# One order for each engine, key columns twice in the weights, fp32 keys transposed and then split, in a fused four-block kernel

## The reference, cut to what matters

```python
def _L0(x, attn_bias, mask, g_in, null_attn_bias, null_kv, Wq, Wkv, Wo, g_out):
    xn = layernorm(x, g_in)
    q = (xn @ Wq).reshape(b, n, H, DH).transpose(0, 2, 1, 3) * scale
    k, v = split(xn @ Wkv)                      # one head of 64 each
    k, v = concat([null_kv[0], k]), concat([null_kv[1], v])
    sim = einsum('bhid,bjd->bhij', q, k) + concat([null_attn_bias, attn_bias])
    sim = where(causal or masked, -max, sim)
    out = einsum('bhij,bjd->bhid', softmax(sim), v)
    return layernorm(out.reshape(b, n, H * DH) @ Wo, g_out)

def _L1(...):   # the same, but q and k are l2-normed and scaled, and the bias is
    h = silu(ln(silu(ln(pos @ w0 + b0, g0)) @ w1 + b1, g1)) @ w2 + b2
    bias = h[i - j + n - 1]

def _L2(hidden, g, wt, wg, w_gate, w_up, w_down, sw_gate, sw_up, sw_down):
    scores = softmax((hidden @ wt.T + repeat(g @ wg.T)) / 2);  top 2 of 8, renormed
    y_all = einsum('etm,emh->eth', leaky(x @ w_gate) * (x @ w_up), w_down)
    return sum of the chosen y_all * weight + leaky(x @ sw_gate) * (x @ sw_up) @ sw_down

x = x + _L0(x, ...); x = x + _L1(x, ...); x = x + _L2(x, ...); x = x + _L3(x, ...)
```

## Time and profile before

| | |
|---|---|
| Runs, us | 355.8, 356.56, 358.19 (median 356.56) |
| Profiled execution, span from first to last instruction, us | 354.29 |
| Median of the runs less that span, us | 2.27 |
| PE busy, us (share) | 326.7 (92%) |
| DVE, ACT, POOL busy, us | 252.7, 245.7, 197.6 |
| PE without work, whole span, us | 27.6 |
| of that in the first 25 us | 5.7 |
| Mean granted TensorE clock | 0.990 |

### The profile page before, as it was taken

One profiled execution on the slowest core, in us unless ns is written; L12 is line 12 of the kernel. 1 busy time (PEld: TensorE's weight loads), 2 busy tenths in 40 slices (PEclk: granted clock), 3 DMA queues, 4 the chain that ended last, 5 costly groups with the idle time before them and its releaser, 6 DMA issues.

```text
span 354.3 us, 7091 instructions
## 1 busy us (share of the span) xinstructions
PE 326.7 (92%) x2276; PEld 247.4 (70%) x2276; DVE 252.7 (71%) x917; ACT 245.7 (69%) x822; POOL 197.6 (56%) x297
## 2 busy tenths in 40 slices
PE   7789999997999999989996899889999899999996
PEld 5676875777686677756685577667767578676885
DVE  4768998795575777858884889578769536477672
ACT  3579886995698688969894889697986922232330
POOL 4591196379527956977596779877953502200000
PEclk9999999998999999999998999999999999999999
DMA  5961202320939401128200202021120200000001
GB/s 178 382 171 42 62 0 64 48 59 1 142 39 150 91 2 37 26 64 345 58 5 2 62 1 61 5 58 31 33 61 2 61 2 0 0 3 0 0 2 59
DMA packets 26653, 21.33 MB, mean 60 GB/s; under 512 B 2436, under 2 KB 25976, under 8 KB 26232
## 3 DMA queue, kind: packets, MB, share of 16 engines
q1 hardware_dynamic: 25624, 20.37, 23.2%
q10 hardware_dynamic: 992, 0.51, 1.1%
HBM read 19.84 MB, written 1.04 MB: 59 GB/s over the span
## 4 chain that ended last, share of the span: by engine, by line
PE 45%; POOL 16%; ACT 13%; DVE 12%; DMA 6%; issue 6%; ACTq 0%; SPq 0%; DVEq 0%; POOLq 0%
PE bank L1422 7%; ACT sb_prob L785 5%; POOL sb_nb L927 5%; POOL sb_oT L933 4%; PE bank L1389 3%; DMA sb_r_rows<-recip_rows 3%; DVE sb_prob L1164 3%; PE bank L1361 3%; PE bank L1414 3%; PE bank L1446 3%; PE bank L1540 3%; PE bank L1536 2%; ACT sb_pT L793 2%; POOL sb_rq L908 2%; PE bank L1502 2%
## 5 line engine op out<-in xcount | busy, mean ns | idle before, releaser
L785 ACT ACTIVATE sb_prob<-sb_prob,sb_low 128x128 f32<-128x128 f32 (+1 forms) x256 | 113.4, 449 | 5.0 <-DVE sb_low L1164 3.9
L793 ACT ACTIVATE sb_pT<-bank 128x512 f32<-128x512 f32 x96 | 54.0, 590 | 10.2 <-PE bank L1414 9.4
L1414 PE MATMUL bank<-sb_ident,sb_prob 128*128 128x128 f32 x384 | 56.4, 281 | 3.4 <-ACT sb_pT L793 1.4
L1414 PEld LDWEIGHTS bank<-sb_ident,sb_prob 128*128 128x128 f32 x384 | 42.2, 141 | 21.2 <-issue 8.3
L1422 PE MATMUL bank<-sb_pT,sb_v_a 128*64 128x512 f32 x192 | 48.3, 609 | 1.9 <-ACT sb_ln L806 1.9
L785 ACT ACTIVATION_READ_ACCUMULATOR sb_prob<-sb_prob,sb_low 128x1 f32 x256 | 49.8, 195 | 0.0
L933 POOL TENSOR_TENSOR sb_oT<-sb_oT,sb_r_rows 128x512 f32<-128x512 f32 x30 | 38.1, 1292 | 13.5 <-DMA sb_r_rows<-recip_rows 12.2
L1164 DVE CUSTOM_DVE_ANT_0 sb_prob<-bank,sb_nb,sb_t 128x128 f32<-128x128 f32 x128 | 38.6, 342 | 9.7 <-PE bank L1389 8.8
L908 POOL TENSOR_TENSOR sb_rq<-sb_ss,sb_minus_half 128x8 f32<-128x8 f32 x16 | 26.4, 1651 | 15.6 <-DVE sb_ss L1131 15.5
L846 ACT ACTIVATE sb_leak<-bank 128x512 f32<-128x512 f32 x20 | 12.0, 598 | 30.2 <-PE bank L1504 30.0
L1446 PE MATMUL bank<-sb_wo,sb_oT 128*128 128x128 f32 x256 | 31.6, 276 | 0.5 <-POOL sb_oT L933 0.4
(11 more groups left out here) (205 smaller groups left out, 772.6 us busy)
## 6 DMA issues: line engine op xcount, KB each, us to landing
sb_r_rows<-recip_rows SPq DMA_DIRECT2D x30, 256.0 KB, 4.1
sb_packed<-in_packed SPq DMA_DIRECT2D x1, 2992.0 KB, 11.9
sb_bias<-in_bias SPq DMA_DIRECT2D x1, 2048.0 KB, 13.3
sb_toep<-bias_table SPq DMA_DIRECT2D x8, 256.0 KB, 9.4
sb_stage<-in_L_cond_Wq SPq DMA_DIRECT2D x2, 512.0 KB, 5.4
sb_bias<-in_bias SPq DMA_DIRECT2D x1, 1024.0 KB, 8.5
sb_wo<-in_L_cond_Wo SPq DMA_DIRECT2D x1, 512.0 KB, 12.4
sb_wo<-in_L_cond_Wout SPq DMA_DIRECT2D x1, 512.0 KB, 7.0
```

The lines of the kernel that those rows point to most:

```text
L785: act.activation(p[:, j], p[:, j], ACT.Exp, scale=-1.0, bias=low[:, buf, half, h:h + 1], accum_out=total[:, buf, half, h:h + 1]).then_inc( ...
L793: act.activation(pT[:, c % PT_SLOTS].rearrange("p j q -> p (j q)"), t_ring.bank("T", s, n)[:], ACT.Copy).then_inc(t_ring.frees("T", s, n), 1)
L1414: ins = pe.transpose(dst[:, j * P:j * P + P], p[:, j % 2, kb * P:kb * P + P], ident[:])
```

## The change

The change has five parts.

1. `AT`, `attention_order` and `ORDER` go. Each engine gets a string of letters, one letter for a kind of step, which gives that engine's own order; the numbers within a kind run up. All engines but SyncE get another order than before. SyncE's loads ahead of the list stay as they are.
2. The weights hold the key columns twice, so `kv` is 208 columns wide in place of 144 (192 in place of 128 for answer 0), and a key arrives twice side by side without a copy. The split of the key-value weights is done in pieces.
3. `kt` transposes the keys in fp32 straight from `sb_kv`, in one step of two transposes in place of two steps of two, and the split into high and low comes behind it: in `ke`, ACT writes the high parts of `sb_k_bd` and `sb_kT` from the bank, DVE the low parts. `sb_k_src`, `sb_kn`, `sb_v_a` and the steps `k_hi` and `k_lo` go. In block 1 a DVE step `k_gain` scales the keys in `sb_kv` in place.
4. `sb_kv` has two buffers, by the answer's parity. `V` reads the values from it. The eviction of `kv` waits for the last `V` of the answer two before.
5. `m_first`, the first step of the experts' down product, becomes part of `m_down`.

```diff
-ORDER = attention_order()
+KV = 3 * DH + H
+QKV = INNER + KV
...
+def in_order(kinds, letters):
+
+    kinds = kinds.split()
+    left = {kind: iter(pieces(kind)) for kind in kinds}
+    named = [kinds[LETTERS.index(letter)] for letter in letters]
+    return [(kind, *next(left[kind])) for kind in named]
...
+ORDERS = {
...
+    "PE": in_order(
+        "xt kv kt q h kvn S T V Z NW ht W table qt m_g m_x m_logits m_weights m_gate m_spread m_down spread",
+        "abcdeddfdgabgdhhgcidghhdighgjhghhkldheiahmhhgjbilhdchggihhggnmhjdihhdhghihdmhhgaijbhhdggichdmhhgghijdhhgai"
...
-    kv = sb("kv", [P, 2, KV])
+    kv = sb("kv", [P, 2, 2, KV])
-    kn = sb("kn", [P, 2, DH])
-    k_src = sb("k_src", [P, 2, 2, 2, DH], F32R)
-    v_a = sb("v_a", [P, 2, 2, DH])
...
-        for kind, s, n in ORDER:
+        for kind, s, n in ORDERS["ACT"]:
...
             if kind == "kv":
                 w.wait_ge(*p_ring.filled("kv", s, 0))
-                if s > 0:
-                    w.wait_ge(t0_made, 2 * s)
-                cols = 2 * DH if s == 0 else KV
-                act.activation(kv[:, :, 0:cols],
+                if s >= 2:
+                    w.wait_ge(t0_made, 2 * (s - 1))
+                    w.wait_ge(*o_ring.filled("V", s - 2, FOURS - 1))
+                cols = 3 * DH if s == 0 else KV
+                act.activation(kv[:, buf, :, 0:cols],
...
-            if kind == "k_hi":
-                w.wait_ge(*p_ring.emptied("kv", s, 0))
-                if lay == 0:
-                    act.activation(k_src[:, :, 0], kv[:, :, 0:DH].unsqueeze(2).to_broadcast([P, 2, 2, DH]), ACT.Copy,
-                                   scale=K_SCALE).then_inc(kv_high, 1)
-                if s >= 2:
-                    w.wait_ge(*o_ring.filled("V", s - 2, FOURS - 1))
-                act.activation(v_a[:, buf], kv[:, :, DH:2 * DH], ACT.Copy)\
-                    .then_inc(kv_high, 1)
...
+                src = t_ring.bank("kt", s, 0)
+                for j in range(2):
+                    rows = slice(j * DH, j * DH + DH)
+                    act.activation(k_bd[rows, 0, j], src[rows, 0:P], ACT.Copy, scale=scale).then_inc(k_high, 1)
+                act.activation(kT[:, buf, 0], src[:, 0:N], ACT.Copy, scale=scale).then_inc(k_high, 1)
...
+            if kind == "ke":
+                scale = K_SCALE if lay == 0 else 1.0
+                src = t_ring.bank("kt", s, 0)
+                w.wait_ge(k_high, 3 * s + 3)
+                for j in range(2):
+                    rows = slice(j * DH, j * DH + DH)
+                    ins = dve.scalar_tensor_tensor(k_bd[rows, 1, j], src[rows, 0:P], scale, k_bd[rows, 0, j].bitcast(F32),
+                                                   ALU.mult, ALU.subtract)
+                ins.then_inc(k_diagonal, 1)
+                dve.scalar_tensor_tensor(kT[:, buf, 1], src[:, 0:N], scale, kT[:, buf, 0].bitcast(F32),
+                                         ALU.mult, ALU.subtract).then_inc(t_ring.frees("kt", s, 0), 1)
...
             if kind == "kt":
-                w.wait_ge(kv_low, s + 1)
-                for part in range(2):
-                    ins = pe.transpose(dst[:, part * P:part * P + P],
-                                       k_src[:, n, part].rearrange("p c d -> p (c d)").bitcast(F32), ident[:])
+                if lay == 0:
+                    w.wait_ge(*p_ring.emptied("kv", s, 0))
+                else:
+                    w.wait_ge(kn_made, s - B + 1)
+                for t in range(2):
+                    ins = pe.transpose(dst[:, t * P:t * P + P], kv[:, buf, t, 0:P], ident[:])
                 ins.then_inc(full, 1)
```

441 lines of the change are left out of this document (123 added, 318 removed).

## The result

In the comparison that goes with the changed kernel it takes 369.65 us (median of four runs, 367.69 to 371.68) and the kernel before 357.38 (355.8 to 358.29): a ratio of 1.036, interval 1.031 to 1.041. It is slower, as forecast, and inside the stated range, but the forecast said +1.5% and it is +3.6%: 369.65 us lies where rival C was put (365 to 372) and not where the forecast's own story was (358 to 366).

The account below looks back on a forecast made before the run. PE was taken to bound the kernel, busy 326.7 of 354.3 us. 354.3 + 9.0 + 0.9 − 1.6 − 7.9 + 5.0 = 359.7 us of span, 2.3 more for the runs: 362.0 us (+1.5%), range 351.5 to 370.

Parts of the forecast that it names:

- rival C: Slower still: all five `W` waits in full and DVE bounding block 0; 367.5 us for the runs, chance 0.24.
- the forecast's own story: Whole kernel: a start that costs ten and is given back in part; 362.0 us, chance 0.49 for 358 to 366.
- The start: First `h` on PE waits for nine small loads until 21.2 us, delaying S.0.2 from 26.90 to 36.1: +9.0 us.
- The clock: PE's idle at the start lowers its granted clock; half of one drop like that at 83 us: +0.9 us.
- PE's own work: On PE, sixteen transposes go (−2.2 us) and 48 `kv` matmuls get 64 columns more (+0.6): −1.6 us.
- Waits that go: PE's waits of `xt` on `norm` (4.6), `kt` on ACT's eviction (2.1) and `kv` on the split (1.2) vanish: −7.9 us.
- Waits that come: PE at `W` waits for the reciprocals' way from `Z` through `scale`, 8.7 us each, at five places: +5.0, between 0 and 8.5.
- ACT and DVE at nothing: Copies leave ACT (about −1.2 us per answer), half the split goes to DVE (+0.5); both costed at nothing.
- Rivals A and B: A: touched waits and both clock drops go, no `W` waits, 353.6 us, 0.19; B: `h` does not wait, 353.1 us, 0.08.

Follow-up runs that it names:

- start2: Changed kernel with the first steps of PE, DVE, ACT and POOL, first `h` among them, in about the sequence of the kernel before: 360.9 us, ratio 1.008.
- best2: start2 with six `scale` steps on POOL and four `W` on PE (with their evictions) moved later: 356.5 us, ratio 0.992 to the kernel before.
- no_rows: Changed kernel, but `scale` multiplies `sb_oT` by itself without waiting for the reciprocals' rows, so the softmax is not normalised: 346.52 us, ratio 0.970.
- w_late: Changed kernel with only four `W` on PE moved later, with their evictions on ACT and DVE: 377.86 us, ratio 1.056 to the kernel before.
- best3: best2 with six more moves of DVE's and ACT's steps: 360.48 us, ratio 1.011 to the kernel before.

## Why the prediction was right in direction and short in size

**The start (+9.0, clock +0.9).** The end of the wait was right to 0.2 us, and start2 wins 8.8 back. That this meets the +9.0 is partly luck, since locally the loss is larger: S.0.2 13.4 us later in place of 9.2, and the first `Z` 15.7. Three parts were not in the working: `kv.0` starts at 10.43, behind DVE's second weight split, 2.0 us later than in the kernel before (8.47); the clock stays down until about 33 us (0.54 from 21 to 35 us), where I had put half of one drop; and the first `min` comes at 35.67 in place of 31.4, since POOL's null term for it waits 2.00 us for ACT's eviction of `kvn`:

```profile
35.38 0.25 POOL L667 TENSOR_TENSOR sb_t<-sb_kv,sb_null_bias 128x32 f32<-128x32 f32 x1 [2.00 <-ACT sb_kv L554]
```

PE was done with `kvn` by 29.2 us, but in ACT's order the eviction stands behind the split of answer 1's `xn`, and that waits until PE transposes it, at 34.33. The path later absorbs some of that: the changed kernel is 15.7 us behind at the first `Z`, 21.6 at the first of answer 2 (123.22 against 101.62), 18.8 at that of answer 7, 15.5 at the end.

**The clock** was the most undersized item where busy time is concerned. best2 has the same 2260 matmuls with a mean clock of 0.990, that of the kernel before, and PE is busy 321.8 us; the changed kernel, at 0.952, 330.5. These 8.7 us are matmuls that ran longer, against +0.9 in the sum. Half of them are W's own, here in the changed kernel and then in best2:

```profile
L1272 PE MATMUL bank<-sb_wo,sb_oT 128*128 128x128 f32 x256 | 36.9, 299 | 13.5 <-POOL sb_oT L738 13.1
```

```profile
L1322 PE MATMUL bank<-sb_wo,sb_oT 128*128 128x128 f32 x256 | 32.4, 278 | 1.4 <-POOL sb_oT L788 1.2
```

And no_rows, whose clock from 21 to 35 us is about as low (0.58), has PE busy only 321.9 us: so most of the 8.7 go with the round trip and not with the start, which is where the sum had looked for the clock. How many of them lie on the path was not isolated.

**PE's own work (−1.6).** Right in sign, too small: at the same clock best2 has 4.9 us less than the kernel before. The groups of instructions give `kt` 3.3 in place of 6.2 us (−2.9, forecast −2.2) and `kv` 13.9 in place of 14.6 (−0.7, forecast +0.6): 64 more columns cost nothing, the bound from below was the better one. The remaining 1.3 lies in groups that the change leaves as they were, whose means differ between two profiles.

**Waits that go (−7.9).** `xt` −4.3 and `kt` −1.7 as forecast; `kv` went the other way (1.2 to 2.0, of which 1.8 at the start). The net is −5.2, 2.7 us short.

**Waits that come (+5.0): the step that failed.** It took the way from `Z` to `W` rightly as too short, and named four of the five W that wait (the second half of answers 1, 4 and 6, the first of 2; the first of 1 waits too, the second of 2 does not). I had 8.5 us as its upper bound; PE stood 13.1. Two things were wrong. The first is the cost of the way, put at 8.7 us five times: from `Z` to `W` these five took 12.5, 10.2, 12.0, 10.3 and 9.3 us, the first three beside transfers of the bias table (last section), the last one held up by DVE's eviction of V as well. The second is the path: "Who waits at `W`: all of PE's queue behind it, and V" leaves out that POOL stands as well. `scale` is in POOL's queue, so the null shares, `norm` and cuts behind it come late, ACT behind them, and PE's T and q behind ACT. no_rows shows what both ways cost together, up to 23 us here against 6 in the kernel before; w_late shows the second way by itself; the two ends moved win 5.5. Rival C named the very sign, "POOL's `scale` starting on the landing of `sb_r_rows` at most answers", and nine such waits came where there had been three, and its price, 367.5, was the nearest. Its other half, DVE bounding block 0, was not shown: DVE is busy 50.00 of 58 us there, less than before.

**ACT and DVE at nothing ("PE's 92% hides them").** DVE's busy time rose by 9.4 us (252.7 to 262.1), where +0.5 per answer makes 4. In the orders as changed nothing speaks against hiding it, DVE waits 0.4 us at `ke`. As a statement on the key path with the orders of before it is wrong: in the two places that were tried that path costs 12.9 and 25.5 us, where the prediction had 355.0 us for it. Work off the bounding engine is hidden only where the order leaves room at that place.

**The sum from the runs.** Start −8.8, both ends of the round trip −5.5, one by one; together 369.65 − 356.5 = 13.2, nearly the 14.3 of the two. With them the change comes out about where the kernel before is (ratio 0.992), so by the medians these two hold the whole of its loss.

In PE's own time, against the kernel before, the 15.5 us of span are: work −4.9, matmuls that ran longer +8.7, the wait at `h` +8.3, the waits at `W` +12.7 (0.4 to 13.1), the three waits of the earlier trace rows −5.2, and all other waits −4.1. The prediction's terms for these were −1.6, +0.9, +9.0, +5.0, −7.9 and nothing; the two that are far too small, the clock and W, both belong to the round trip in the main.

Rivals A and B fell: nothing like the 8.3 us that A needed was given back, and `h` waited. On the room, the page of the changed kernel without round trip and with early loads has PE busy 321.5 of 338.7 us, 95%, with the weight loads at 74%. The Trainium skill ("Perfetto Trace Analysis", "Identifying the Most-Contended Engine") takes the second number, beside the FLOPs done, for the nearness to the limit, and not the first. No run here decides between them: a span can't be shorter than the busy time in it, and this one still has 17 us of other time.

Still open: what share of the start is clock; whether the three long trips would be short with the bias table's transfers at another time, which no run moved; why best3's moves lost 4 us beyond the one wait shown; and what the old key path would cost in the new orders, which was not tried.
